# A convolution done on TensorE by shifted matmuls in a Mamba, attention and experts kernel, with first dA's between the norms and the experts' layers in another order

## What is computed

```python
# block 1, x = x + block(group_norm(x)); per sample 25 sequences (j) of T = 32 steps, 256 inner channels
xz = einsum('btc,ec->bte', xr, W_in);  xc, z = split(xz, 2)
xp = pad(xc, 3 steps in front)
xc = silu(sum over k of xp[:, k:k + T, :] * conv_w[:, k] + conv_b)          # 4 taps along t
x_dbl = xc @ W_xproj.T                       # dt_in (16), B (16), C (16)
dt = softplus(dt_in @ W_dt.T + b_dt);  A = -exp(A_log)
h = exp(dt * A) * h + (dt * xc) * B;  y = sum over 16 states of h * C        # scan over t
y = (y + xc * D_skip) * silu(z);  out = rmsnorm(y @ W_out.T) * ln_w + res
# block 2, t = t + relu(attention(layer_norm(t)) @ proj_w + proj_b), 8 heads of 16
# block 3, t = t + experts(layer_norm(t)): routing per sample over 8 experts, the top 2 of them,
#          each gelu(x @ W1 + b1) @ W2 + b2, then a layer norm
```

## Time and profile before

| | |
|---|---|
| median of 3 runs | 1883.69 us (1883.29 to 1889.07) |
| profiled execution, its own time | 1883.54 us |
| its span | 1881.9 us |
| PE matmul busy | 1193.2 us, 63% |
| DVE busy | 1426.9 us, 76% |
| ACT busy | 1085.5 us, 58% |
| POOL busy | 629.3 us, 33% |
| DMA, mean | 97 GB/s |
| mean granted TensorE clock | 0.82 of full speed |

### The profile page before, as it was taken

How to read it: one execution, slowest core, us unless ns; L and a number is a source line. 1 busy time by engine, 2 the same in 40 slices (tenths; PEclk the granted TensorE clock), 3 DMA queues, 4 the chain that set the end, 5 groups by cost and what they waited for, 6 DMA issues and landing times. The chain is left out here.

```text
span 1881.9 us, 21900 instructions
## 1 busy us (share of the span) xinstructions
PE 1193.2 (63%) x7072; PEld 518.3 (28%) x7072; DVE 1426.9 (76%) x2371; ACT 1085.5 (58%) x1985; POOL 629.3 (33%) x364
## 2 busy tenths in 40 slices
PE   4115377855785478638873788377846773883883
PEld 2002132232223222313232323232222222322773
DVE  4796888878887887889878888888878873602685
ACT  3333557674777378636864676657675762672330
POOL 2363325423351335231533153325422441000344
PEclk9556688977897789868995889679977896897997
DMA  2430633055304631271217140733054303102551
GB/s 58 153 135 11 196 66 123 19 192 99 115 27 156 135 106 36 102 188 44 98 38 219 35 131 13 222 66 124 18 194 88 123 20 85 22 1 81 151 135 47
DMA packets 88344, 182.13 MB, mean 97 GB/s; under 512 B 15442, under 2 KB 42894, under 8 KB 88238
## 3 DMA queue, kind: packets, MB, share of 16 engines
q1 hardware_dynamic: 85950, 174.27, 32.4%
q0 software_dynamic: 1408, 3.29, 0.7%
q10 hardware_dynamic: 880, 3.28, 0.6%
HBM read 143.61 MB, written 36.86 MB: 96 GB/s over the span
## 5 line engine op out<-in xcount | busy, mean ns | idle before, releaser
L1145 DVE TENSOR_TENSOR_SCAN hst<-dA,PS 128x800 f32<-128x800 f32 x256 | 466.1, 1821 | 115.1 <-ACT dA L851 95.1
L887 ACT ACTIVATE probs<-PS 128x400 f32<-128x400 f32 x800 | 341.8, 524 | 101.5 <-PE PS L1448 100.5
L851 ACT ACTIVATE dA<-dt_rep,a_sb 128x775 f32<-128x775 f32 x256 | 242.7, 951 | 172.4 <-DVE hst L1145 168.0
L1448 PE MATMUL PS<-q_stack,k_stack 99*128 99x400 bf16 (+1 forms) x896 | 234.4, 355 | 89.4 <-ACT probs L887 47.3
L877 ACT ACTIVATE probs<-PS 128x400 f32<-128x400 f32 x400 | 201.7, 504 | 137.2 <-PE PS L1415 115.3
L1138 DVE TENSOR_TENSOR PS<-u_rep,b_rep 128x800 f32<-128x800 f32 x256 | 267.7, 1046 | 16.4 <-DMA u_rep<-u_dram 5.7
L733 POOL TENSOR_TENSOR dt_sb<-hst,c_rep 128x800 f32<-128x800 f32 x88 | 165.5, 1881 | 340.4 <-DVE PS L1138 340.4
L1172 DVE CUSTOM_DVE_ANT_0 probs<-PS,probs 128x400 f32<-128x400 f32 x400 | 219.2, 573 | 45.7 <-issue 18.7
L733 POOL TENSOR_TENSOR sp_l<-hst,c_rep 128x800 f32<-128x800 f32 x88 | 165.6, 1881 | 153.9 <-DVE PS L1138 134.2
L1433 PE MATMUL PS<-probs,v_ext 128*32 128x400 f32 (+1 forms) x1792 | 200.6, 525 | 14.5 <-DVE o_raw L1193 8.9
L1414 PE MATMUL PS<-k_stack,q_stack 96*128 96x400 bf16 (+1 forms) x448 | 143.9, 357 | 97.1 <-DVE k_neg L1167 97.1
(11 more groups left out here) (214 smaller groups left out, 1894.8 us busy)
## 6 DMA issues: line engine op xcount, KB each, us to landing
b_rep<-b_dram SPq DMA_DIRECT2D x64, 400.0 KB, 3.8
c_rep<-c_dram SPq DMA_DIRECT2D x64, 400.0 KB, 4.0
dt_rep<-dt_dram SPq DMA_DIRECT2D x64, 400.0 KB, 6.1
u_rep<-u_dram SPq DMA_DIRECT2D x64, 400.0 KB, 6.4
q_stack<-parts_dram SPq DMA_DIRECT2D x96, 100.0 KB, 5.4
k_stack<-parts_dram SPq DMA_DIRECT2D x96, 100.0 KB, 6.8
dt_dram<-dt_sb SPq DMA_DIRECT2D x16, 400.0 KB, 3.6
u_dram<-sp_l SPq DMA_DIRECT2D x16, 400.0 KB, 3.5
```

The costliest lines, as they stand in the source:

```text
L851: nc.scalar.activation(dA[:, i % 2, :].rearrange("p (j t) -> p j t", t=T)[:, :, 1:T], dt_rep[:, gi, :].rearrange("p (j t) -> p j t", t=T)[ ...
L887: nc.scalar.activation(probs[:, j % NPROB, :], bank(4 + j % 3, HALF), ACT.Exp, scale=ATT_SCALE).then_inc(probs_ready.sem, 1)
L1145: nc.vector.tensor_tensor_scan(hst[:, i % 2, :], dA[:, i % 2, :], dbu, 0.0, ALU.mult, ALU.add).then_inc(scan_done.sem, 1)
L1448: last = nc.tensor.matmul(bank(4 + j % 3, HALF)[strip], k_stack[:, h, kt * P:kt * P + strip.stop - strip.start], q_stack[:, h, q0:q0 + HAL ...
```

## The change

**Convolution within the in-projection.** A convolution along t with four taps, of a matmul's result, is the sum of four matmuls whose weights are scaled by a tap each and whose input columns are shifted by 0, 25, 50 and 75. DVE forms the four scaled copies of the x half of W_in once, in the prologue (w_conv_sb, from two tiles that live in the memory of z_act and hst), behind a wait for all weights that now stands ahead of its first group norm. The taps are loaded spread over all partitions (512 KB). `project_and_convolve` issues eight matmuls for each half. ACT's silu reads PSUM and adds the bias. `convolve` on DVE is gone, with its two waits.

**Another order in the front.** PE does both x halves first, x_project, and then the z halves with the first dt projection between them; the two x halves stand in banks 2 and 4, the z halves in 0 and 4; the transposes of the attention output go to bank 6. ACT's order follows.

**First dA between the norms.** ACT forms dA of steps 0 and 1 in the front, between norm 2 and norm 1, and no longer in `steps`.

**Experts.** PE does the first layer of sample b + 1 before the second layer of sample b, written out for the 8 samples instead of a loop.

```diff
@@ PE @@
-            def project_in(b, e):
-                return over_spans(b, w_in_sb[:, e * P:(e + 1) * P], xnT)
+            def project_z(b, ck):
+                return over_spans(b, w_z_sb[:, ck * P:(ck + 1) * P], xnT)
+
+            def project_and_convolve(b, ck):
+                for at, width in SPANS:
+                    for back in range(TAPS):
+                        lo = max(at, back * J)
+                        last = nc.tensor.matmul(PS[:, b * BANK + lo:b * BANK + at + width],
+                                                w_conv_sb[:, TAPS - 1 - back, ck * P:(ck + 1) * P],
+                                                xnT[:, lo - back * J:at + width - back * J],
+                                                start=(back == 0), stop=(back == TAPS - 1))
+                return last
...
-                    project_in(2, 0).then_inc(xz_up.sem, 1)
+                    else:
+                        pe.wait_ge(w_conv_ready, 1)
+                    project_and_convolve(2, 0).then_inc(xz_up.sem, 1)
...
+                    project_and_convolve(4, 1).then_inc(xz_up.sem, 1)
+                if f is not None:
+                    pe.wait_ge(silu_done.sem, silu_done.at(f, 1))
+                    x_project(0)
+                if f is not None:
+                    pe.wait_ge(silu_done.sem, silu_done.at(f, 2))
+                    x_project(1).then_inc(xd_up.sem, 1)
                 if n is not None:
                     pe.wait_ge(oT_ready.sem, oT_ready.at(n, 1))
                     over_spans(6, proj_w_sb[:, :], oT).then_inc(proj_up.sem, 1)
                 if f is not None:
-                    pe.wait_ge(silu_done.sem, silu_done.at(f, 2))
-                    x_project(0)
+                    if m is not None:
+                        pe.wait_ge(y_summed.sem, y_summed.at(m, NC_))
+                    project_z(0, 0).then_inc(xz_up.sem, 1)
+                    pe.wait_ge(xd_ready.sem, xd_ready.at(f, 1))
+                    over_spans(2, w_dt_sb[DT0:P, 0:P], xd[DT0:P, :]).then_inc(dt_up.sem, 1)
+                    project_z(4, 1).then_inc(xz_up.sem, 1)
@@ ACT @@
-                    act.wait_ge(conv_done.sem, conv_done.at(f, ck + 1))
-                    nc.scalar.activation(in_jt(xc[:, ck, :]), by_tj(sp_e[:, ck, :]), ACT.Silu).then_inc(silu_done.sem, 1)
+                    act.wait_ge(xz_up.sem, xz_up.at(f, ck + 1))
+                    nc.scalar.activation(in_jt(xc[:, ck, :]), by_tj(wide((2, 4)[ck])), ACT.Silu,
+                                         bias=conv_b_sb[:, ck:ck + 1]).then_inc(silu_done.sem, 1)
...
+                if f is not None:
+                    for i in range(2):
+                        decay(f, i)
                 if m is not None:
                     act.wait_ge(ln1_std.sem, ln1_std.at(m, 1))
                     norm_apply(norm1, t1, ln1_tok).then_inc(ln1_ready.sem, 1)
@@ DVE @@
+            dve.wait_ge(weights_in, NW[0])
+            for k in range(TAPS):
+                last = nc.vector.tensor_tensor(w_conv_sb[:, k, :], w_x_raw, taps_raw[:, :, k], ALU.mult)
+            last.then_inc(w_conv_ready, 1)
...
-                if f is not None:
-                    convolve(0)
...
-                if f is not None:
-                    convolve(1)
@@ PE, experts @@
+            first_layer(0)
+            for bt in range(B):
+                if bt + 1 < B:
+                    first_layer(bt + 1)
+                second_layer(bt)
```

More of the change, by code:

```diff
@@ L153, in mamba_attention_moe @@
         a_raw = over(u_rep, NC_ * NG * NS, k=NC_ * NG, s=NS)
+        w_x_raw = over(z_act, DI, e=DI)
+        taps_raw = over(hst, DI * TAPS, e=DI, k=TAPS)
         a_own = over(dt_rep, NC_ * NG * NS, q=NC_ * NG * NSG, s=SG)
@@ L491, in _ @@
             load_x(0)
-            load(w_in_sb[:, :], w_in_t)
-            load(conv_w_sb[:, :, :], conv_w.rearrange("(c p) k -> p c k", p=P))
+            load(w_x_raw, w_in_t[:, 0:DI])
+            load(taps_raw, conv_w.unsqueeze(0).to_broadcast([P, DI, TAPS]))
+            load(w_z_sb[:, :], w_in_t[:, DI:2 * DI])
             load(conv_b_sb[:, :], conv_b)
@@ L831, in front @@
                     norm_apply(norm2, t2, f_tok).then_inc(ln2_ready.sem, 1)
+                if m is None and f is not None:
+                    act.wait_ge(a_ready, 1)
+                if f is not None:
+                    for i in range(2):
+                        decay(f, i)
                 if m is not None:
@@ L838, in front, with decay @@
                                          accum_out=x_mean[:, n:n + 1]).then_inc(fT_ready.sem, 1)
-                if m is None and f is not None:
-                    act.wait_ge(a_ready, 1)
+            def decay(m, i):
+                ck, sg, gi, rnd = step(i)
+                if sg == 0:
+                    act.wait_ge(dt_in[gi].sem, dt_in[gi].at(m, 16 * (ck + 1)))
+                if i >= 2:
+                    act.wait_ge(scan_done.sem, scan_done.at(m, i - 1))
+                nc.scalar.activation(dA[:, i % 2, :].rearrange("p (j t) -> p j t", t=T)[:, :, 1:T],
+                                     dt_rep[:, gi, :].rearrange("p (j t) -> p j t", t=T)[:, :, 1:T],
+                                     ACT.Exp, scale=a_sb[:, ck * NG + gi, sg:sg + 1]).then_inc(dA_ready.sem, 1)
             def steps(n, m, f):
                 for i in range(NSTEP):
[L844 to L853, removed]
+                    if m is not None and i >= 2:
+                        decay(m, i)
                     if n is not None:
@@ new lines, in second_layer @@
+            def second_layer(bt):
+                n, z = divmod(bt, 2)
+                pe.wait_ge(h_ready[z].sem, h_ready[z].at(n, TOPK * FC))
+                pe.wait_ge(e_w2_scaled[z].sem, e_w2_scaled[z].at(n, 1))
+                pe.wait_ge(res_read[z].sem, res_read[z].at(n, 0))
+                for kt in range(NT):
+                    o = (4 + 2 * z) * BANK + kt * C
+                    for i in range(TOPK * FC):
+                        last = nc.tensor.matmul(PS[0:TT, o:o + C], hidden[z][i][:, kt * TT:(kt + 1) * TT], w2_s[z][:, i // FC, i % FC, :],
+                                                start=(i == 0), stop=(i == TOPK * FC - 1))
+                last.then_inc(y_e_up[z].sem, 1)
```

91 lines of the change are left out of this document (31 added, 60 removed).

## The result

The changed kernel takes **1923.03 us** (median of 4 runs, 1922.06 to 1924.85), the kernel before 1885.95 us on the same chip (4 runs, 1883.29 to 1889.07): a ratio of 1.018, 95% interval 1.016 to 1.020. It is slower, as forecast, but by 12 us more than the 1911 forecast; 1923.03 stands at the very end of the range (1898 to 1923), level with its upper bound. The spans of the profiled executions are 1922.2 and 1881.9 us, the mean granted clocks 0.816 and 0.82.

A forecast was written before the change was run, and what follows sets the result against it. No engine is busy throughout; a serial front between turns' scans, its chain on DVE, was taken to decide. Six fronts 21.6, turn 0 -2.1, prologue 5.6, experts 2.6 sum to 27.7 over 1883.5: 1911 us, range 1898 to 1923.

The forecast's parts named there:

- rival (a): Full fronts: late dt_rep landings or table costs hold ACT's dA 1 and norm 1; +0.5 to +1.5 each, 1914 to 1920, chance 0.15.
- Full fronts, +3.6 predicted: Six full fronts: u 4.8 us later, less 1.25 for the moved dA's, so 50.4 us each, +21.6 in all.
- up at t = 22.2: Full front: PE's attention-output transposes done 22.2 us after the last scan, before at 13.2, holding t2 on DVE.
- ACT 2.8 late against DVE's 4.8: Full front: ACT's Ln ends 2.8 us later than before, DVE's u 4.8 later, so DVE sets the delay.
- rival (b): Full fronts: DVE's blockage costs no more than ACT's lateness, +2.8 - 1.25 each; 1899 us, chance 0.13.
- (c): Convolution on PE: a matmul costs by its start, four taps cost one, 1.6 us; 1868 us, chance 0.04.
- (d): Full fronts: the t2 block is hidden, fronts only gain 1.25 us at their end; 1882 us, chance 0.06.
- (e): Full fronts: PE runs at 1.2 GHz, a half costs 10.2 us, six fronts +83; 1972 us, chance 0.02.
- Turn 0, -2.1 predicted: Front of turn 0: no t2, so no blockage, and the moved dA's gain; -2.1 us, bounds -3 and 0.
- Prologue, +5.6 predicted: Prologue: DVE waits for all weights before its norm, PE starts 7.8 us late, 2.2 given back; bounds 4 and 9.
- Experts, +2.6 predicted: Experts' start: sample 1's first layer before sample 0's second delays DVE's start by 1.7 to 3.5 us, taken as +2.6.
- from 1737.8: Experts: PE's layer 1 of sample 1 starts at 1737.8 us and ends near 1743.2, ahead of sample 0's layer 2.

## Why the prediction was right, and where it was short

- **Direction and mechanism: right; that the time fell inside the range: in part luck.** The forecast's own bounds were +-7 us, to 1918. The range reached up to 1923 only for rival (a), which did not come about; 12 us of other misses, all of one sign, took its place.
- **Signs.** All appeared: t2 waits for PE (13.14 us; some 10 were forecast), the dt ReLU for nothing, the first scan for the transposes, the first convolution starts near 23.6 (24.08).
- **Full fronts, +3.6 predicted, +4.05 measured; 2.7 us of the miss.** The step that was off is "up at t = 22.2": it was 23.0. A half costs 5.36 us where 5.1 was reckoned from columns, and silu with bias from PSUM 1.69 and 1.61 where 1.57 was taken. The two z halves and dt 0 took 4.4 us from start to start where 4.0 were reckoned, and the x path gained 0.3 us (the xd copy began at 1394.75, t = 16.4, against 16.7 before) instead of 0.7. So u came 5.3 later instead of 4.8. The dA term held (1.25 predicted; 1.3 by two runs).
- **ACT 2.8 late against DVE's 4.8: right in its sense.** Ln ended at 1406.42, t = 28.1: 3.5 late against DVE's 5.3. With the transposes 3 us earlier the front gained only 0.85, in part since dt 0 then came 0.9 us later. So rival (b) is out: the full fronts lost 4.05 us and not 1.55.
- **Late landings (rival a): no.** The second dA waited 0.31 us for dt_rep (at most 0.39 in the six full fronts) and still ended 1.18 us ahead of norm 1's scale. In turn 0's front it waited 2.18 us and still ended 0.60 us ahead of it. The other rivals are out by the same rows; that a matmul costs by its start (c) by 5.36 us for a half, no change (d) by the 13.14 us for which t2 waits, PE at 1.2 GHz (e) by the same 5.36 us.
- **The table load.** It takes 1.28 us and dA follows 1.30 behind its start, as in the earlier trace rows. The drain of the Trainium skill (ScalarE: Activation LUTs, What ACT_TABLE_LOAD costs) doesn't show. By that rule the moved dA's would have ended at t = 44.0; they ended at 42.8.
- **Turn 0, -2.1 predicted, -1.15 measured.** PE stayed at 1.2 GHz for longer: conv 0 took 7.62 us there, 6.9 was reckoned. The front of turn 0 before had work at 1.2 GHz too: it is 3.6 us longer than in the kernel with only its dA's moved, and these are worth 1.2.
- **Prologue, +5.6 predicted, +6.8 measured.** The four products took 2.19 us together (1.6 reckoned), PE started 0.5 later than predicted, and the chain behind it gave back 1.4 us instead of 2.2.
- **Experts, +2.6 predicted, +5.7 measured and 0.8 behind; the largest term of the miss, 3.9 us.** The failed step is "from 1737.8": it let sample 1's first layer start where PE became free. It started 1.96 us later, behind a DMA of that sample, and took 7.33 us where 5.4 were reckoned. The second of these is the granted clock, 0.77: at 1.00 the layer took 5.67 us in two other profiles, and the start cost 3.0 to 3.4 us there, near the forecast. I priced the order by what PE does and did not ask when the operands of the work pulled forward arrive. The 0.8 us behind lie within the scatter of that stretch.
- **Turn 8's front, 0 predicted, +2.95 measured.** No instruction moved there. PE's clock fell earlier (last section).

Together 2.7 + 0.95 + 1.2 + 3.9 + 2.95, and 0.9 in the steps, are the 12.6 us between 27.7 and 40.3. By these rows some 4.5 us of that (full fronts, prologue, the experts' start at full clock) are terms of the mechanism sized too low, an estimate; some 5.4 (2.95, and 2.3 to 2.7 at the experts) are the clock in the execution profiled; the rest is turn 0 and scatter of the steps and of the end.

## What to carry to other kernels

Work moved from a busy engine to a less busy one is paid at the place where it lands: here 8 us left DVE, but lay largely beside other work (only 1.3 us a front were to be had in this order), and 7.5 us came onto PE in front of everything the front waits for. Then look at the in-order queue of each waiting engine for what stands ahead of the critical instruction, and at when the operands of work pulled forward arrive. And a wait taken away at one point (2.2 us before the scan) is worth only what the next consumer of the same result does not wait for.

## What the runs showed of the hardware

TensorE's granted clock differs between the profiled executions in places where nothing was changed. With one profile of each kernel it can't be told whether it is the kernel or the execution that decides. The stretch from 150 to 160 us behind the last scan, the end of turn 8's attention, holds the same PE work in all kernels. These are windows of before (1693.61) and of the changed kernel (1724.45); columns: window, length, busy time and instructions of PE, its weight loads, DVE, ACT and POOL, then PE's granted clock as a share of 2.4 GHz, the DMA share and GB/s.

```profile
1693.61:1703.61 10.00, 6.01 (x44) 3.32 (x36) 2.58 (x9) 1.03 (x2) 0.00 (x0) 1.00 0.00 0
```

```profile
1724.45:1734.45 10.00, 6.25 (x42) 4.00 (x35) 2.58 (x9) 0.82 (x1) 0.00 (x0) 0.81 0.01 2
```

The clock fell to 1.2 GHz within this stretch in the changed kernel, but only behind it in the kernel before. The projection of the attention output there, before and changed:

```profile
1701.76 1.61 PE L1283 MATMUL PS<-part_rest,proj_w_sb 128*128 128x512 f32 x4 [0.92 <-ACT part_rest L805]
```

```profile
1733.16 3.03 PE L1281 MATMUL PS<-part_rest,proj_w_sb 128*128 128x512 f32 x4 [0.92 <-ACT part_rest L811]
```

With the transposes ahead of it (0.90 and 1.59 us) and behind it (1.08 and 1.95) that makes 3.0 us, the whole of the difference: the way to the experts took 189.76 instead of 186.81 us. It was 186.8 to 186.9 with the dA's back in the steps and with one tap, 189.5 to 189.7 with the moved dA's alone or with the last wait away, the late scaling, the experts' loop and the transposes moved, and 191.6 with the convolution alone (in the last two of these profiles a part was lost nearer the scan): no part of the change goes with it. Likewise in the prologue of the kernel before with moved dA's the second x projection took 3.03 us instead of 1.61, and the first scan came 3.0 us later; with the last wait away, where the prologue's code is the same, it took 1.61. So at each of these two sparse stretches of PE some 3 us hung on when the clock fell, which no reading of the order would have told; what decides it stays open.
